# Two layers' norms with their short chains on GpSimd, and block-diagonal keys filled by 16 transfers a unit

## The chip, the cores and the metric

The kernel runs on one core of one Trainium2 chip (8 cores). A core has TensorE (PE, with its weight loads PEld), VectorE (DVE), ScalarE (ACT), GpSimd (POOL) and SyncE (SP, which issues transfers here). Each runs its own instructions in order, and semaphores tie them together. The metric is the device time of one execution in microseconds, the median of several.

## The reference

x is (16 sequences, 512 positions, 256 wide), and passes through six residual blocks, each on a layer-normed input:

```python
x = x + L0_attn(layernorm(x))    # rms norm, three gates by matmul, linear recurrence along positions, output matmul
x = x + L0_xattn(layernorm(x), ctx, ctx, mask)     # 16 heads of 16, 64 context keys
x = x + L0_ffn(layernorm(x))     # 256 -> 256 plus a rank-32 correction
x = x + L1_attn(layernorm(x))    # LSTM of width 20 over positions -> where to look, Gaussian weights, context
x = x + L1_xattn(layernorm(x), ctx, ctx, fside, mask)  # softmax times fside
x = x + L1_ffn(layernorm(x))     # each row goes to the best of 8 experts, 256 -> 128 -> 256

def _layernorm(x, eps=1e-05):
    return (x - mean(x)) / sqrt(var(x) + eps)

def _L0_attn_ref(x, norm_w, A_w, ...):
    xn = x * (norm_w / sqrt(mean(x * x) + EPS))
```

Scores, softmax and the sums are all in float32.

## The kernel before, in words

Positions are cut into 4 chunks of 128, sequences into 4 groups of 4; a chunk of a group is a unit (128 partitions x 4 sequences x 256). Each of the two layers has 16 units. Two lanes, each with its own tiles (names begin with l0 and l1, norms' tiles with ln0 and ln1; the profile leaves the numbers out), work on two units at once. Stages follow each other: in stages 0 and 1 both lanes run layer 0 (two bodies of two units each); in stages 2 and 3 lane 0 runs layer 0 and lane 1 layer 1 (four bodies each); in stage 4 lane 1 runs layer 1 (four bodies); in stage 5 both lanes run layer 1 (two bodies); stage 6 finishes the experts. The LSTM steps along the positions run beside stages 1 to 4: 64 steps a body in stage 1, 32 in stages 2 to 4. Each step is a chain of L942 on TensorE (slots in, gates out), L1109 and L1113 on ScalarE, and L1641 to L1649 on VectorE, which writes slots for the next step. The experts' tiles run in stages 4 to 6.

The order of the work is not written by hand. `norm_steps`, `attention_steps`, `layer0_steps` and others list steps (engine, family, index, cost in us, what it needs). `planned_at` (from L351) lists them out per engine by their costs and by the hop between engines, and `run_stages` emits each engine's share of that list. Where the plan has TensorE idle by over 0.3 us in stages 0 to 4 and 6, it puts in filler matmuls "warm" (L950), one for each 0.22 us of 0.9 of the gap. So a changed cost in a step changes the order on every engine, and the number of fillers.

A norm (each unit of layer 0 has four, of layer 1 two) is: statistics in two halves on VectorE (L1348 to L1353), variance plus epsilon on VectorE (L1357), the power −0.5 on GpSimd (L1697), the offset −mean x scale on VectorE (L1373), then two tiles normed by ScalarE (L1126) and two by VectorE (L1450). The first norm of layer 0 folds layernorm and rms norm in one scale and has `rms` (L1359 to L1369) and a second root between; its input is xin.

The scores of two sequences' heads are one matmul per half (L909): the queries against keys laid out block-diagonally, so that head e's 16 rows meet only its own 64 columns. Before, `load_context` (L726 to L742) loads plain keys kg (L737) once a unit, and GpSimd multiplies them with headmask into one of two 128x512 buffers kbd, eight times a unit (`keys`, L1712). GpSimd also adds the output's bias rows to the residual (`brow`, `frow`, `orow`, L1665), multiplies layer 1's exponents by fside (`gate`, L1719), copies rows for the LSTM's slots (L1677), and gathers rows for the experts. SyncE issues x, contexts, histories, stores and the experts' loads.

## Time and profile before

| what | value |
|---|---|
| time, median of 3 | 2620.91 us (2616.39 to 2623.07) |
| profiled execution, its time | 2631.95 us |
| its span | 2629.8 us |
| TensorE busy | 2302.6 us, 88% |
| VectorE, ScalarE, GpSimd busy | 60%, 54%, 40% |
| mean granted clock of TensorE | 0.947 |

The profile comes from one execution that is 11 us slower than the median. The span runs from the first to the last instruction. Busy time is a union of an engine's instructions; a filler counts as busy. From the timeline, the loop bodies end at about 220 and 355 us (stage 0), 524 and 692 (stage 1), 843, 986, 1130 and 1273 (stage 2), 1411, 1546, 1682 and 1820 (stage 3), 1930, 2032, 2138 and 2242 (stage 4), 2400 and 2560 (stage 5).

### The profile page before, as it was taken

To read this page: it belongs to the slowest core of one execution; us is meant where nothing else is said; L and a number is where in the kernel's file an instruction comes from. 1 tells how busy PE (TensorE), PEld (TensorE's weight loads), DVE (VectorE), ACT (ScalarE), POOL (GpSimd) and SP (SyncE) were. 2 spreads that over 40 slices of the span, in tenths; PEclk is the share of its full clock that TensorE was granted. 3 is DMA by queue.
4 is the path that set the end of the run, shared out by engine and by line. 5 is a ranking of instruction groups with operands and counts; after the bars stand their busy time and mean duration, and the time that the engine had idled before them with its cause. 6 is when DMAs were issued, how large, how long until landed. Compare 5 with 4: busy or idle time off the path is not lost.

```text
span 2629.8 us, 42733 instructions
## 1 busy us (share of the span) xinstructions
PE 2302.6 (88%) x11585; PEld 1499.8 (57%) x11585; DVE 1578.0 (60%) x5494; ACT 1425.8 (54%) x5145; POOL 1046.3 (40%) x1124
## 2 busy tenths in 40 slices
PE   5799999999899898989898989798888878697887
PEld 2365655656556564747465655556655546566664
DVE  4456477676665766666576767676645646364541
ACT  1263646658464554737474747464655646465632
POOL 0223241232233433333334343433555545487665
PEclk9899999999899999989899999998999999798989
DMA  4302020100302011111203030302353243353323
GB/s 161 99 11 64 14 62 1 51 9 1 94 9 70 17 53 35 46 49 30 48 17 94 1 95 0 86 16 81 103 126 97 78 121 90 112 163 98 92 62 105
DMA packets 203923, 168.32 MB, mean 64 GB/s; under 512 B 56847, under 2 KB 196717, under 8 KB 203452
## 3 DMA queue, kind: packets, MB, share of 16 engines
q1 hardware_dynamic: 189372, 140.73, 18.6%
q0 software_dynamic: 14336, 25.28, 3.3%
q8 instruction: 67, 1.10, 0.2%
q14 instruction: 148, 1.21, 0.2%
HBM read 125.11 MB, written 53.40 MB: 68 GB/s over the span
## 4 chain that ended last, share of the span: by engine, by line
PE 37%; issue 24%; DVE 16%; POOL 12%; ACT 5%; SPq 3%; DMA 2%; POOLq 0%; DVEq 0%; another core or an unknown queue 0%; ACTq 0%
PE p L970 7%; PE p L950 4%; PE p L873 4%; PE p L933 3%; PE p L909 3%; POOL l_scratch L1719 3%; PE p L867 3%; PE p L884 2%; PE pg L942 2%; PE p L923 2%; DVE l_xnat L1450 2%; POOL l_kbd L1712 2%; POOL l_xres L1665 2%; DVE ln_stats L1348 1%; PE p L1023 1%
## 5 line engine op out<-in xcount | busy, mean ns | idle before, releaser
L1161 ACT ACTIVATE l_scratch<-p,l_mx 128x64 f32<-128x64 f32 x2048 | 483.4, 323 | 30.8 <-DVE l_mx L1395 20.2
L950 PE MATMUL p<-warm 128*128 128x512 bf16 x1802 | 476.1, 394 | 1.2 <-DVE l_sums L1343 1.2
L1712 POOL TENSOR_TENSOR l_kbd<-l_kg,headmask 128x512 f32<-128x512 f32 x256 | 264.1, 1044 | 385.0 <-PE p L909 289.6
L942 PEld LDWEIGHTS pg<-slots,wcat 128*128 128x128 f32 x1024 | 174.7, 197 | 287.6 <-DVE slots L1649 218.6
L1697 POOL TENSOR_TENSOR ln_rstd<-ln_ve,neghalf 128x4 f32<-128x4 f32 x96 | 98.2, 1022 | 547.2 <-DVE ln_ve L1357 545.1
L942 PE MATMUL pg<-slots,wcat 128*128 128x16 f32 x1024 | 180.9, 252 | 125.7 <-DVE slots L1649 105.0
L933 PEld LDWEIGHTS p<-l_vg,l_scratch 128*128 128x128 f32 x2048 | 254.4, 193 | 62.3 <-ACT l_scratch L1169 37.7
L950 PEld LDWEIGHTS p<-warm 128*128 128x128 bf16 x1802 | 185.4, 107 | 173.5 <-issue 40.0
L933 PE MATMUL p<-l_vg,l_scratch 128*128 128x34 f32 x2048 | 264.0, 276 | 6.8 <-ACT l_scratch L1169 4.5
L909 PE MATMUL p<-l_kbd,l_qT 128*128 128x512 f32 x512 | 265.4, 600 | 0.6 <-POOL l_kbd L1712 0.5
L1719 POOL TENSOR_TENSOR l_scratch<-l_scratch,gp 128x512 f32<-128x512 f32 x128 | 162.5, 1270 | 221.3 <-DVE l_sums L1400 219.8
L1395 DVE TENSOR_REDUCE l_mx<-p 128x8 f32<-128x512 f32 x256 | 176.2, 690 | 93.9 <-PE p L909 86.8
L1641 DVE SCALAR_TENSOR_TENSOR pg<-gates,pg 20x16 f32<-20x16 f32 x512 | 89.8, 175 | 214.0 <-ACT gates L1109 194.1
L1109 ACT ACTIVATE gates<-pg 96x16 f32<-96x16 f32 x512 | 92.0, 180 | 219.9 <-PE pg L942 208.3
L867 PE MATMUL p<-ident,l_xnat 128*128 128x128 f32 x1024 | 158.4, 291 | 40.1 <-ACT l_xnat L1126 36.6
L1169 ACT ACTIVATE l_scratch<-p 128x512 f32<-128x512 f32 x256 | 153.6, 600 | 52.7 <-PE p L923 44.8
L1113 ACT ACTIVATE pg<-pg 20x16 f32<-20x16 f32 x512 | 77.3, 151 | 191.0 <-DVE pg L1645 179.5
L923 PE MATMUL p<-ident,l_scratch 128*128 128x128 f32 x1024 | 159.0, 282 | 22.7 <-DVE l_xnat L1410 16.8
L867 PEld LDWEIGHTS p<-ident,l_xnat 128*128 128x128 f32 x1024 | 124.6, 151 | 85.6 <-ACT l_xnat L1126 65.1
L1126 ACT ACTIVATE l_xnat<-l_xres,ln_shift,ln_rstd 128x256 f32<-128x256 f32 x160 | 87.1, 592 | 154.9 <-DVE ln_shift L1373 153.7
L923 PEld LDWEIGHTS p<-ident,l_scratch 128*128 128x128 f32 x1024 | 120.8, 148 | 81.2 <-issue 40.5
L1649 DVE SCALAR_TENSOR_TENSOR slots<-gates,pg 20x16 f32<-20x16 f32 x528 | 88.8, 171 | 104.8 <-ACT pg L1113 93.0
(281 smaller groups left out, 4381.7 us busy)
## 6 DMA issues: line engine op xcount, KB each, us to landing
xln<-xln_dram SPq DMA_DIRECT2D x40, 512.0 KB, 4.7
l_vg<-v_dram SPq DMA_DIRECT2D x32, 544.0 KB
x_dram<-l_xres SPq DMA_DIRECT2D x32, 512.0 KB, 4.2
l_kg<-k_dram SPq DMA_DIRECT2D x32, 256.0 KB
xln_dram<-l_xnat SPq DMA_DIRECT2D x16, 512.0 KB, 3.0
l_xres<-x_dram SPq DMA_DIRECT2D x16, 512.0 KB
x_dram<-l_xnat SPq DMA_DIRECT2D x16, 512.0 KB
xin<-in_x SPq DMA_DIRECT2D x12, 512.0 KB, 3.8
```

Source lines behind the costliest of these rows:

```text
L867: i = pe.transpose(banks[l][m][:, b * P:(b + 1) * P], src[:, b, m * P:(m + 1) * P], ident[:, :])
L909: pe.matmul(banks[l][j], w.qT[:, j, b * P:(b + 1) * P], w.kbd[b % 2][:, j, :, :].rearrange("p a k -> p (a k)"), start=False, stop=True).th ...
L923: i = pe.transpose(t_bank[l][:, p * P:(p + 1) * P], src, ident[:, :])
L933: i = pe.matmul(o_of(l, layer, c)[:, q * VW:(q + 1) * VW], w.exT[:, j, p, :], w.vg[:, b, q * VW:(q + 1) * VW], start=True, stop=True)
L942: pe.matmul(pg[:, 0:B], wcat[:, :], slots[:, s % STEPS, :], start=True, stop=True).then_inc(l_pe, 1)
L950: pe.matmul(banks[1][0] if layer > NC_ else px, warm[:, 0:P], warm[:, :], start=True, stop=True)
L970: i = pe.matmul(bank, w[:, k, half * P:(half + 1) * P], tiles[lane].xT[:, k, :], start=(k == 0), stop=(k == NH - 1))
L1161: i = act.activation(w.ex[b % 2][:, NE * j + h, :], banks[lane][j][:, h * SK:(h + 1) * SK], ACT.Exp, scale=-1.0, bias=w.mx[:, u % 4, h:h + 1])
L1169: act.activation(w.exT[:, i_ % 2, :, :], t_bank[lane].rearrange("p (a t) -> p a t", a=4), ACT.Identity).then_inc(t.exT, 1)
L1395: dve.tensor_reduce(w.mx[:, u % 4, :], banks[l][j].rearrange("p (a k) -> p a k", a=NE), AX_X, ALU.min).then_inc(t.top, 1)
L1712: pool.tensor_tensor(w.kbd[b % 2][:, j, :, :], w.kg[:, j, b:b + 1, :].broadcast_to([P, NE, SK]), headmask[:, :].rearrange("p (a o) -> p a ...
L1719: pool.tensor_tensor(ex, ex, gp[lane][:, b:b + 1, :].broadcast_to([P, NE, SK]), ALU.mult).then_inc(t.gated, 1)
```

## The change

What it does:

- All small operations of a norm between statistics and norm go to GpSimd: four for a plain norm (plus epsilon, power, mean x scale, x −1), eleven for layer 0's first. VectorE keeps statistics and its half of the norm.
- The plan's costs: 1.75 for a root with its chain and 4.2 for `rms` (before, 1.0 for a root, 1.2 for rms, 0.2 or 0.35 for the offset).
- kg, headmask and `keys` are gone. kbd is one tile of 128x4096 a lane, cleared once by VectorE at the start, and its diagonal blocks are written by 16 transfers a unit (one head of one half each: 16 partitions x 4 sequences x 64), 16 KB each. The score matmuls wait for them once a unit. The next context load now waits for all of the unit's scores.
- `brow` also waits for VectorE's half of the first norm; `orow` waits for the fourth score.
- Tiles move to make room: some of the experts' tiles lie in the columns of R, one of xg in the rows of the biases.

Filler matmuls in one body (first body of a stage / body of its loop), as the two programs have them:

| stage | before | after |
|---|---|---|
| 0 | 95 | 103 |
| 1 | 142 | 140 |
| 2 | 106 / 120 | 111 / 126 |
| 3 | 70 / 76 | 68 / 69 |
| 4 | 61 / 109 | 65 / 109 |
| 5 and 6 | 176 | 176 |

The diff, cut to its core:

```diff
+LOADS = (16 * (NE * NH + 1), 16 * (NE * NH + 2))
...
-        self.kg = sb(f"{name}_kg", [P, NH, GB, SK])
-        self.kbd = [sb(f"{name}_kbd{i}", [P, NH, NE, SK]) for i in range(2)]
+        self.kbd = sb(f"{name}_kbd", [P, GB, NH, NE, SK])
...
-    steps = [("dve", "stat", 2 * k + h, 1.2, after[h:h + 1]) for h in range(2)]
-    steps += [("pool", "root", k, 1.0, [("stat", 2 * k + 1)])]
-    if rms:
-        steps += [("dve", "rms", 0, 1.2, [("root", k)]), ("pool", "root", 9, 1.0, [("rms", 0)])]
-    steps += [("dve", "offset", k, 0.35 if rms else 0.2, [("root", 9 if rms else k)])]
-    steps += [("act", "norm", 2 * k, 1.2, [("offset", k)]), ("dve", "norm", 2 * k + 1, 1.0, [("offset", k)])]
+    steps = [("dve", "stat", 2 * k + h, 1.15, after[h:h + 1]) for h in range(2)]
+    steps += [("pool", "rms" if rms else "root", k, 4.2 if rms else 1.75, [("stat", 2 * k + 1)])]
+    ready = ("rms" if rms else "root", k)
+    steps += [("act", "norm", 2 * k, 1.2, [ready]), ("dve", "norm", 2 * k + 1, 1.0, [ready])]
...
-            ("pool", "keys", u, 1.07, [("score", u - 4)]),
-            ("pe", "score", u, 1.1, [("qland", u % 2), ("keys", u), ("neg", 0), ("exp", 4 * (u - 2) + 3)]),
+            ("pe", "score", u, 1.1, [("qland", u % 2), ("neg", 0), ("exp", 4 * (u - 2) + 3)]),
...
-    steps += [("pool", "orow", 0, 2.3, [("keys", 7)])]
+    steps += [("pool", "orow", 0, 2.3, [("score", 3)])]
...
-    steps += [("act", "base", 0, 2.4, [("rms", 0)]), ("pool", "brow", 0, 2.3, [("base", 0)]),
+    steps += [("act", "base", 0, 2.4, [("rms", 0)]), ("pool", "brow", 0, 2.3, [("base", 0), ("norm", 1)]),
...
-                    sp.wait_ge(t.kbd, 2 * GB * m)
+                    sp.wait_ge(t.scores, 2 * GB * m)
                     sp.wait_ge(t.pv, 2 * GB * m)
                     sp.wait_ge(t.neg, m)
                     if layer == 1 and m > LAYER0_UNITS[lane]:
                         sp.wait_ge(t.gated, 2 * GB * (m - LAYER0_UNITS[lane]))
                 sp.dma_start(w.vg[:, :, :], v_dram[layer, bass.ds(GB * g, GB), :, :].rearrange("b p n -> p b n")
                              ).then_inc(t.v_load, 16)
-                sp.dma_start(w.kg[:, :, :, :], k_dram[layer, :, :, bass.ds(GB * g, GB), :]).then_inc(t.m_load, 16)
+                for e in range(NE):
+                    rows = slice(HD * e, HD * e + HD)
+                    for h in range(NH):
+                        sp.dma_start(w.kbd[rows, :, h, e, :], k_dram[layer, rows, h, bass.ds(GB * g, GB), :]).then_inc(t.m_load, 16)
...
-                    pe.wait_ge(t.kbd, N + 1)
+                    if u == 0:
+                        pe.wait_ge(t.m_load, LOADS[0] * n + LOADS[0] if layer == 0 else LOADS[0] * LAYER0_UNITS[l] + LOADS[1] * n + LOADS[1])
                     pe.matmul(banks[l][j], w.qT[:, j, b * P:(b + 1) * P],
-                              w.kbd[b % 2][:, j, :, :].rearrange("p a k -> p (a k)"), start=False, stop=True
+                              w.kbd[:, b, j, :, :].rearrange("p a k -> p (a k)"), start=False, stop=True
...
-                    act.wait_ge(s.offset, s.before(layer, n, k) + 1)
+                    act.wait_ge(s.inv, s.before_roots(layer, n, k) + (4 if k else 8))
...
+            for t in tiles:
+                dve.memset(t.kbd[:, :, :, :, :], 0.0)
...
-            def rms(s, small, roots):
-
-                dve.wait_ge(s.inv, roots + 1)
-                dve.tensor_tensor(s.tmp[:, 0, :], s.rstd[:, 0, :], s.rstd[:, 0, :], ALU.mult).then_inc(s.small, 1)
-                dve.wait_ge(s.small, small + 6)
-                dve.tensor_tensor(s.tmp[:, 1, :], s.tmp[:, 0, :], s.mv[:, :, 1], ALU.mult).then_inc(s.small, 1)
-                dve.wait_ge(s.small, small + 7)
-                dve.tensor_scalar(s.ve[:, 1, :], s.tmp[:, 1, :], EPS, None, ALU.add).then_inc(s.small, 1)
-
-                dve.scalar_tensor_tensor(s.tmp[:, 2, :], s.mv[:, :, 0], -1.0, s.rstd[:, 0, :], ALU.mult, ALU.mult).then_inc(s.small, 1)
-                dve.tensor_scalar(s.tmp[:, 0, :], s.rstd[:, 0, :], 1.0, None, ALU.add).then_inc(s.small, 1)
...
-                dve.scalar_tensor_tensor(s.shift[:, :], s.mv[:, :, 0], -1.0, scale, ALU.mult, ALU.mult).then_inc(s.offset, 1)
...
-                    dve.wait_ge(s.offset, s.before(layer, n, k) + 1)
+                    dve.wait_ge(s.inv, s.before_roots(layer, n, k) + (4 if k else 8))
...
-                    elif i_ == 9:
-                        pool.wait_ge(s.small, s.before_small(0, n, 0) + 8)
-                        pool.tensor_tensor(s.rstd[:, 1, :], s.ve[:, 1, :], neghalf[:, :], ALU.pow).then_inc(s.inv, 1)
                     else:
-                        pool.wait_ge(s.small, s.before_small(layer, n, i_) + 5)
-                        if i_ == 0 and positive(n):
-                            pool.wait_ge(s.normed_act, s.before(0, n, 0))
-                            pool.wait_ge(s.normed_dve, s.before(0, n, 0))
+                        done = s.before_roots(layer, n, i_)
+                        pool.wait_ge(s.small, s.before_small(layer, n, i_) + 4)
+                        pool.tensor_tensor(s.ve[:, 0, :], s.mv[:, :, 1], eps4[:, :], ALU.add).then_inc(s.inv, 1)
+                        pool.wait_ge(s.inv, done + 1)
                         pool.tensor_tensor(s.rstd[:, 0, :], s.ve[:, 0, :], neghalf[:, :], ALU.pow).then_inc(s.inv, 1)
+                        pool.wait_ge(s.inv, done + 2)
+                        pool.tensor_tensor(s.tmp[:, 1, :], s.mv[:, :, 0], s.rstd[:, 0, :], ALU.mult).then_inc(s.inv, 1)
+                        pool.wait_ge(s.inv, done + 3)
+                        pool.tensor_tensor(s.shift[:, :], s.tmp[:, 1, :], minus4[:, :], ALU.mult).then_inc(s.inv, 1)
+                elif family == "rms":
+                    done = s.before_roots(0, n, 0)
+                    pool.wait_ge(s.small, s.before_small(0, n, 0) + 4)
+                    if positive(n):
+                        pool.wait_ge(s.normed_act, s.before(0, n, 0))
+                        pool.wait_ge(s.normed_dve, s.before(0, n, 0))
+                        pool.wait_ge(l0.base_ready, n)
+                    pool.tensor_tensor(s.ve[:, 0, :], s.mv[:, :, 1], eps4[:, :], ALU.add).then_inc(s.inv, 1)
+                    pool.wait_ge(s.inv, done + 1)
+                    pool.tensor_tensor(s.rstd[:, 0, :], s.ve[:, 0, :], neghalf[:, :], ALU.pow).then_inc(s.inv, 1)
+                    pool.wait_ge(s.inv, done + 2)
+                    pool.tensor_tensor(s.tmp[:, 0, :], s.rstd[:, 0, :], s.rstd[:, 0, :], ALU.mult).then_inc(s.inv, 1)
+                    pool.wait_ge(s.inv, done + 3)
+                    pool.tensor_tensor(s.tmp[:, 1, :], s.tmp[:, 0, :], s.mv[:, :, 1], ALU.mult).then_inc(s.inv, 1)
+                    pool.wait_ge(s.inv, done + 4)
+                    pool.tensor_tensor(s.ve[:, 1, :], s.tmp[:, 1, :], eps4[:, :], ALU.add)
+                    pool.tensor_tensor(s.tmp[:, 3, :], s.mv[:, :, 0], minus4[:, :], ALU.mult).then_inc(s.inv, 1)
+                    pool.wait_ge(s.inv, done + 5)
+                    pool.tensor_tensor(s.rstd[:, 1, :], s.ve[:, 1, :], neghalf[:, :], ALU.pow).then_inc(s.inv, 1)
+                    pool.wait_ge(s.inv, done + 6)
+                    pool.tensor_tensor(s.tmp[:, 4, :], s.rstd[:, 0, :], s.rstd[:, 1, :], ALU.mult).then_inc(s.inv, 1)
+                    pool.wait_ge(s.inv, done + 7)
+                    pool.tensor_tensor(s.shift[:, :], s.tmp[:, 3, :], s.tmp[:, 4, :], ALU.mult).then_inc(s.inv, 1)
+                    pool.tensor_tensor(s.tmp[:, 2, :], s.tmp[:, 3, :], s.rstd[:, 0, :], ALU.mult).then_inc(s.inv, 1)
+                    pool.tensor_tensor(s.tmp[:, 0, :], s.rstd[:, 0, :], minus4[:, :], ALU.subtract).then_inc(s.inv, 1)
                 elif family == "brow":
                     pool.wait_ge(l0.base_ready, n + 1)
+                    pool.wait_ge(s.normed_dve, s.before(0, n, 0) + 1)
...
+                    pool.wait_ge(t.scores, 2 * GB * m + 4)
...
-                elif family == "keys":
-                    if i_ == 0:
-                        pool.wait_ge(t.m_load, 32 * n + 32 if layer == 0 else 32 * LAYER0_UNITS[lane] + 48 * n + 48)
-                    if positive(N - 3):
-                        pool.wait_ge(t.scores, N - 3)
-                    pool.tensor_tensor(
-                        w.kbd[b % 2][:, j, :, :], w.kg[:, j, b:b + 1, :].broadcast_to([P, NE, SK]),
-                        headmask[:, :].rearrange("p (a o) -> p a o", o=1).broadcast_to([P, NE, SK]), ALU.mult
-                    ).then_inc(t.kbd, 1)
```

How the order changes, first on GpSimd, at the head of a loop body of stage 2 (l0 is layer 0's lane, l1 layer 1's; ln0 is lane 0's norm; L1697 and L1691 are the two roots of the first norm, L1665 is the first row addition). Before:

```order
L1712 TENSOR_TENSOR l0_kbd0<-l0_kg,headmask 128x512
...
L1697 TENSOR_TENSOR ln0_rstd<-ln0_ve,neghalf 128x4
...
L1734 TENSOR_TENSOR l1_scratch<-l1_scratch,below 128x512
...
L1712 TENSOR_TENSOR l1_kbd0<-l1_kg,headmask 128x512
...
L1691 TENSOR_TENSOR ln0_rstd<-ln0_ve,neghalf 128x4
L1712 TENSOR_TENSOR l0_kbd0<-l0_kg,headmask 128x512
...
L1712 TENSOR_TENSOR l1_kbd1<-l1_kg,headmask 128x512
...
L1665 TENSOR_TENSOR l0_xres<-l0_xres,rowOut 128x1024
...
L1677 COPY slots<-R 96x128
L1712 TENSOR_TENSOR l0_kbd1<-l0_kg,headmask 128x512
L1712 TENSOR_TENSOR l1_kbd1<-l1_kg,headmask 128x512
...
L1688 TENSOR_TENSOR pos1_nrm<-pos1_nrm,neghalf 128x4
```

After:

```order
L1650 COPY slots<-R 96x128
...
L1679 TENSOR_TENSOR ln0_ve<-ln0_mv,eps4 128x4
...
L1681 TENSOR_TENSOR ln0_rstd<-ln0_ve,neghalf 128x4
...
L1683 TENSOR_TENSOR ln0_tmp<-ln0_rstd 128x4
...
L1685 TENSOR_TENSOR ln0_tmp<-ln0_tmp,ln0_mv 128x4
...
L1687 TENSOR_TENSOR ln0_ve<-ln0_tmp,eps4 128x4
...
L1690 TENSOR_TENSOR ln0_rstd<-ln0_ve,neghalf 128x4
...
L1692 TENSOR_TENSOR ln0_tmp<-ln0_rstd 128x4
...
L1694 TENSOR_TENSOR ln0_shift<-ln0_tmp 128x4
...
L1726 TENSOR_TENSOR l1_scratch<-l1_scratch,below 128x512
...
L1650 COPY slots<-R 96x128
...
L1638 TENSOR_TENSOR l0_xres<-l0_xres,rows0 128x1024
```

Before, five key products stand between the roots and around the row addition; afterwards the chain runs in one piece, behind two slots copies, and the row addition comes later than it.

On VectorE, the same place: from the mask's conversion to the norm of xin. pg, uin and slots are the LSTM's. Before:

```order
L1387 TENSOR_SCALAR l0_neg<-mask8_0 128x256
...
L1362 TENSOR_TENSOR ln0_tmp<-ln0_rstd 128x4
...
L1364 TENSOR_TENSOR ln0_tmp<-ln0_tmp,ln0_mv 128x4
...
L1366 TENSOR_SCALAR ln0_ve<-ln0_tmp 128x4
L1368 SCALAR_TENSOR_TENSOR ln0_tmp<-ln0_mv,ln0_rstd 128x4
L1369 TENSOR_SCALAR ln0_tmp<-ln0_rstd 128x4
...
L1641 SCALAR_TENSOR_TENSOR pg<-gates,pg 20x16
...
L1458 TENSOR_TENSOR ln0_tmp<-ln0_rstd 128x4
...
L1373 SCALAR_TENSOR_TENSOR ln0_shift<-ln0_mv,ln0_tmp 128x4
...
L1450 TENSOR_SCALAR l0_xnat<-xin,ln0_mv,ln0_tmp 128x256 x2
```

After:

```order
L1371 TENSOR_SCALAR l0_neg<-mask8_0 128x256
...
L1374 TENSOR_SCALAR l1_neg<-mask32_1 128x256
...
L1614 SCALAR_TENSOR_TENSOR pg<-gates,pg 20x16
...
L1616 SCALAR_TENSOR_TENSOR uin<-gates,pg 20x16
...
L1618 SCALAR_TENSOR_TENSOR pg<-pg,uin 20x16
L1622 SCALAR_TENSOR_TENSOR slots<-gates,pg 20x16
...
L1432 TENSOR_SCALAR l0_xnat<-xin,ln0_mv,ln0_tmp 128x256 x2
```

The rms chain and the offset between the mask's conversion and the norm are gone; one LSTM step stands between them.

On SyncE, the loads of the first two units ahead of the first loop body. Before:

```order
L724 DMA xin<-in_x 128x4x256
L735 DMA l0_vg<-v_dram 128x4x272
L737 DMA l0_kg<-k_dram 128x2x256
L739 DMA mask8_0<-in_mask0 128x4x64
L724 DMA xln1<-in_x 128x4x256
...
L737 DMA l1_kg<-k_dram 128x2x256
```

After:

```order
L720 DMA xin<-in_x 128x4x256
L731 DMA l0_vg<-v_dram 128x4x272
L736 DMA l0_kbd<-k_dram 16x4x64 x16
L738 DMA mask8_0<-in_mask0 128x4x64
L720 DMA xln1<-in_x 128x4x256
...
L736 DMA l1_kbd<-k_dram 16x4x64 x16
```

The load of lane 1's x (xln1) now stands behind 16 key transfers of lane 0 instead of one.

## Rows read from the trace of the kernel before

**Rows 1.** The profile page, part 1: busy time and share of each engine.

```profile
PE 2302.6 (88%) x11585; PEld 1499.8 (57%) x11585; DVE 1578.0 (60%) x5494; ACT 1425.8 (54%) x5145; POOL 1046.3 (40%) x1124
```

**Rows 2.** Windows, one loop body each: length, busy (instructions) by engine, clock, DMA share, GB/s.

```profile
220.00:355.00 135.00, 133.87 (x627) 83.42 (x626) 76.74 (x230) 73.82 (x212) 41.51 (x33) 1.00 0.15 47
524.00:692.00 168.00, 160.72 (x785) 98.83 (x784) 118.78 (x482) 104.44 (x402) 42.06 (x37) 1.00 0.11 33
986.00:1130.00 144.00, 129.59 (x641) 82.60 (x640) 92.42 (x317) 80.66 (x302) 50.79 (x46) 0.95 0.15 41
1546.00:1682.00 136.00, 121.92 (x608) 79.31 (x606) 94.44 (x317) 82.96 (x303) 50.69 (x47) 0.95 0.15 46
2032.00:2138.00 106.00, 87.93 (x480) 58.00 (x479) 60.07 (x232) 57.53 (x231) 54.81 (x70) 0.97 0.34 99
2400.00:2560.00 160.00, 131.66 (x680) 95.82 (x679) 74.15 (x229) 84.07 (x262) 104.29 (x126) 0.88 0.30 84
```

**Rows 3.** Groups by line and form: busy us, mean ns, idle before, releasers.

```profile
L1712 POOL TENSOR_TENSOR l_kbd<-l_kg,headmask 128x512 f32<-128x512 f32 x256 | 264.1, 1044 | 385.0 <-PE p L909 289.6 <-DMA mask<-in_mask 95.2
...
L1719 POOL TENSOR_TENSOR l_scratch<-l_scratch,gp 128x512 f32<-128x512 f32 x128 | 162.5, 1270 | 221.3 <-DVE l_sums L1400 219.8
...
L1697 POOL TENSOR_TENSOR ln_rstd<-ln_ve,neghalf 128x4 f32<-128x4 f32 x96 | 98.2, 1022 | 547.2 <-DVE ln_ve L1357 545.1
...
L1450 DVE TENSOR_SCALAR l_xnat<-l_xres,ln_mv,ln_rstd 128x256 f32<-128x256 f32 x160 | 63.0, 436 | 2.0
...
L1450 DVE TENSOR_SCALAR l_xnat<-xin,ln_mv,ln_tmp 128x256 f32<-128x256 f32 x24 | 51.4, 2183 | 1.0
...
L1373 DVE SCALAR_TENSOR_TENSOR ln_shift<-ln_mv,ln_rstd 128x4 f32<-128x4 f32 x80 | 31.0, 387 | 35.3 <-POOL ln_rstd L1697 33.2
...
L1754 POOL TENSOR_TENSOR held<-neghalf 1x1 f32<-1x1 f32 x96 | 17.8, 185 | 54.7 <-DVE xy L1607 52.5 <-issue 0.8
```

**Rows 4.** Timeline of 976 to 1016 us: start, duration, instruction, [idle before <-releaser].

```profile
975.70 4.48 PE L950 MATMUL p<-warm 128*128 128x512 bf16 x20
...
980.18 2.68 DVE L1373 SCALAR_TENSOR_TENSOR ln_shift<-ln_mv,ln_rstd 128x4 f32<-128x4 f32 x1 [3.63 <-POOL ln_rstd L1697]
980.80 2.03 POOL L1712 TENSOR_TENSOR l_kbd<-l_kg,headmask 128x512 f32<-128x512 f32 x2
...
990.62 1.01 POOL L1697 TENSOR_TENSOR ln_rstd<-ln_ve,neghalf 128x4 f32<-128x4 f32 x1 [7.78 <-DVE ln_ve L1357]
...
996.51 0.29 DVE L1387 TENSOR_SCALAR l_neg<-mask 128x256 bf16<-128x256 uint8 x1
...
1002.40 5.72 DVE L1450 TENSOR_SCALAR l_xnat<-xin,ln_mv,ln_tmp 128x256 f32<-128x256 f32 x2
...
1009.16 0.60 PE L942 MATMUL pg<-slots,wcat 128*128 128x16 f32 x2 [4.34 <-DVE slots L1649]
...
1014.85 1.53 PE L970 MATMUL p<-l_xT,wD 128*128 128x512 f32 x3
```

**Rows 5.** Timeline of VectorE before the first loop body.

```profile
2.65 4.27 DVE L1268 MEMSET xg<- 128x512 f32 x8
...
28.52 0.61 DVE L1281 TENSOR_SCALAR wA<-wA,normw 128x256 f32<-128x256 f32 x2 [12.39 <-DMA wms<-in_W_mu_sig]
```

**Rows 6.** Timeline of the start of the first loop body, 84 to 110 us.

```profile
85.50 0.62 SPq L737 DMA_DIRECT2D l_kg<-k_dram  x1
...
86.83 0.55 SPq L724 DMA_DIRECT2D xln<-in_x  x1
...
93.04 0.75 DVE L1348 BATCH_NORM_STATS2 ln_stats<-xln 128x6 f32<-128x256 f32 x2 [9.99 <-DMA xln<-in_x]
...
95.61 2.04 POOL L1712 TENSOR_TENSOR l_kbd<-l_kg,headmask 128x512 f32<-128x512 f32 x2 [95.17 <-DMA mask<-in_mask]
...
105.08 0.48 DVE L1387 TENSOR_SCALAR l_neg<-mask 128x256 bf16<-128x256 uint8 x2
```

**Rows 7.** Timeline of SyncE's queue, the context loads of stage 2.

```profile
1094.82 0.53 SPq L737 DMA_DIRECT2D l_kg<-k_dram  x1
```

58 lines of the change are left out of this document (22 added, 36 removed).

## The prediction

> **What bounds the kernel now.** I read the busy shares first, then each stage's loop body by windows, then the timeline of one body engine by engine, and the groups by line last. TensorE is busy for 2302.6 of 2629.8 us [rows 1]. That is an average. A body of stage 0 leaves it idle for 1.1 us of 135, one of stage 1 for 7.3 of 168, of stage 2 for 14.4 of 144, of stage 3 for 14.1 of 136, of stage 4 for 18.1 of 106, of stage 5 for 28.3 of 160 (length less busy time, [rows 2]). And its busy time is not all work: the planner puts filling matmuls into gaps that it expects, 0.22 us each (20 in 4.48 us, [rows 4]), and an in-order engine does them whether the gap comes or not. So the time moves only by (a) waits inside the idle microseconds, (b) the number of fillers, and (c) the run up to the first body. GpSimd is busy for 40%, VectorE for 60% [rows 1]: neither is the bound by its sum. They matter by latency, where one norm's chain stands before TensorE's next work.
>
> One such place is the head of a stage-2 body [rows 4]. The root is through at 991.63 (990.62 + 1.01), the norm by VectorE starts at 1002.40 and takes 5.72 us for two tiles, where the same form on xres takes 0.44 us each [rows 3], so about 4.85 us are a stall. Because VectorE is stuck there, the LSTM's cell update comes late, and TensorE waits for 4.34 us at 1009.16. The norm's user, the wD product, runs at 1014.85. What stands on GpSimd there are key products, the row addition and a copy for the LSTM's slots (the order of before is in the section on the change). The same shape stands at 980.18: an operation on 4 columns takes 2.68 us on VectorE, beside two key products on GpSimd that together take 2.03 us; the group's mean is 0.387 [rows 3].
>
> That is a rule of the Trainium skill too, "SBUF — State Buffer", section "SBUF: two separate sides": VectorE and GpSimd share a pair of ports under an exclusive lock held for the whole instruction, so the loser is blocked and not slowed. The 2.68 us above agrees for operations with two SBUF inputs. By that rule alone, GpSimd's removed keys free VectorE, while its new short operations block it by at most one short operation at a time.
>
> **The change, part by part.** The sum is against the profiled execution: 2629.8 us span, 2631.95 us its time, 11 above the median 2620.91.
>
> *1. Keys off GpSimd.* 256 products of 1.044 us go, 264.1 us in all [rows 3], 8.3 per unit. They were seldom waited for by TensorE itself; their worth is that VectorE is no longer blocked and that roots and row additions no longer queue behind them.
>
> *2. The norm's chain onto GpSimd.* A plain norm has 4 operations there, the first norm of layer 0 has 11. Roots keep 1.022 us each [rows 3]. The price of a 128x4 product there is in no row. The nearest are 1x1 in 0.185 and 128x512 in 1.044 [rows 3]: (1044 − 185) / 511 = 1.7 ns a column, so 0.19 us for 4 columns. The low end is 0.185, the high end is that of the 128x4 power, 1.022. I take 0.19, since power is the odd operation. With a hop of some 0.05 us each, a plain chain is 1.02 + 3 × 0.24 = 1.7 us, and the first norm's 2 × 1.02 + 9 × 0.24 = 4.2. Before, VectorE's part cost 0.17 to 1.23 us an operation with stalls and needed a hop between engines each time. Unstalled, a plain norm is therefore even or 0.2 us later; where VectorE was occupied it is earlier. The first norm of the stage-2 body: from root through (991.63) to norm (1002.40) 10.8 us go down to about 3.2, plus what stands before it.
>
> *3. What that gives TensorE per body.* Stage 2 and 3: the 4.34 us wait goes, and of the 2.68 us stall 2.5 go, 6.8 in all; one us comes back as fillers change and something else is late next (the LSTM's own chain, 32 steps a body, whose gates, cell and slots hop between three engines and stay as they are). I take −6 a body. The low end is −1.5 (the LSTM hides nearly all), the high end −10 of the 14 idle. Eight bodies: −48 (−80 to −12). Fillers in the two stages' bodies: stage 2 from 106 and 120 to 111 and 126, stage 3 from 70 and 76 to 68 and 69 (the counts in the two programs, first and further bodies): +1.3 and −1.5 us a body, which nearly cancel and are in the −6.
> Stage 1: 7.3 us idle a body, −4 each, −8 (−16 to 0). Stage 0: no idle time to win, and 8 more fillers a body × 0.22 = 1.8 us each: +3 (0 to +7), less than the full 3.5 because a filler may stand where TensorE would wait. Stage 4: the experts' weights and the row gathers share SyncE's queue and the DMA engines (share 0.34, [rows 2]); +1 a body, +4 (−6 to +14). Stage 5: gate products of 1.270 us [rows 3] stay on GpSimd, keys go, 28.3 us idle: −3 a body, −6 (−18 to +6).
>
> *4. Row additions.* The first now waits for VectorE's norm 1. Behind it on GpSimd stand the position root and the next norm's chain, so a late VectorE norm delays them; by point 2 that norm is 7 us earlier, so I price this at nothing. If the cover is gone, it costs what the norm is late: 1 to 2 us a body.
>
> *5. Loads.* One load of the keys, 0.62 us to issue [rows 6], becomes 16. The issue alone of the 15 more is at 0.44 (0.53 to 0.62 for rows of whole tiles [rows 6, 7], a little less for small ones, an estimate) 6.6 us of SyncE per unit; ends 0.4 and 0.67: 6 and 10. In the loop it is hidden: the context of stage 2's next body is issued at 1094.82 [rows 7] and its first reader, the mask's conversion, ran at 996.51 in this body [rows 4], hence about 1140 in the next, 45 us later. At the start it isn't. Lane 0's key load is issued at 85.50, lane 1's x at 86.83, and VectorE's first statistics wait 9.99 us for that x until 93.04 [rows 6]. They will start about 6.6 us later. Then GpSimd did two key products before the root (2.04 us at 95.61), which are gone: +4.6. I take +5 (+4 to +9). VectorE's mask conversion at 105.08 comes 16 issues of either lane later, about 107, which the shifted start hides.
>
> The 16 transfers are 16 KB each, in pieces of 256 bytes where the old had 1 KB. Against this speaks a rule of the Trainium skill, "DMA: Bandwidth & Descriptors", section "Rules for kernel authors": coalesce small transfers, since under 64 KB most of the time is overhead. No row here shows such a transfer. What it would do to this kernel is rival B.
>
> *6. The memsets.* Two of 128x4096 on VectorE, less one of 128x512. At 4.27 us for 8 of 128x512 [rows 5] that is 15 × 0.53 = 8.0 us. They stand before a wait of 12.39 us for the last weight load [rows 5], which hides them (one load fewer there, 0.4 us earlier): 0. Uncovered they would cost 8.
>
> **The sum.** +5 + 3 − 8 − 48 + 4 − 6 = −50: 2631.95 → 2582 profiled, 2571 on the scale of the median.
>
> **The rivals.**
> *Rival A, hidden.* TensorE's order, the fillers and the LSTM set the time, and other waits take the place of the 4.34 us. For it: most of the wait in a body is for the slots of the LSTM, and stage 0 gets longer. Against: the wait at 1009.16 ends by an operation queued behind the blocked norm. Eight bodies at −1.5 are −12, stage 1 and 5 give 0, the start +5, stage 0 +3, stage 4 +4: 0, or 2621; with stages 1 and 5 at half their terms −7, or 2614.
> *Rival B, the queue, slower.* In stage 4 and 5 SyncE also issues the experts' loads, x loads and stores. Each unit adds 15 issues. If a small transfer backs the queue up to over 1 us per issue, 16 us stand ahead of the x load and the experts' weights, and TensorE waits for them. Place: stage 4's four bodies (16 us × 4 = 64 at most, some 40 uncovered), the start (+15), stage 5 (+12); the rest of the sum remains: 40 + 15 + 12 on 2571 is 2638. It decides from about 1 us per issue. Against: 0.62 us was the price of the 256 KB one.
> *Rival C, dear small operations.* GpSimd's 4-column product costs about 1 us like its power. A plain chain is then 4.2 us and the first norm's 11.7, so a unit's norms come 3 × 2.5 + 7.5 = 15 us later in all. If 3 of these 15 are exposed, 32 units give +96 on 2571: 2667. Against: the 1x1 product's 0.185.
>
> **How the numbers follow.** What a measurement of this kernel can tell from no change is 0.3%, 8 us. Forecast (2545 to 2600) 0.60; a larger gain, all idle time of stages 2 to 3 and more in 5, under 2545, 0.12; rival A 0.14, of which 0.05 still faster by over 8 us and 0.09 within; rival B 0.09; rival C 0.05. Faster 0.77, same 0.09, slower 0.14. The range 2530 to 2616 leaves out the slower cases, a part of A and the end of the large gain; the forecast's own range is 2545 to 2600.
>
> **What would show each step.** GpSimd's busy time falls from 1046 to about 860 us (−264, + some 77 for the small operations). A 4-column product there takes about 0.19 us; over 0.5 makes C right. VectorE's norm pair on xin takes under 1 us in place of 5.7. TensorE's 4.34 us wait for slots at the head of stage 2's bodies is gone, and bodies of stage 2 take 136 to 139 us, stage 3 129 to 132. Stage 0's bodies are 135 to 137. The first body starts VectorE's statistics near 99 to 100 us. An issue of a key load takes 0.4 to 0.6 us; near 1 or above, or bodies of stage 4 over 110 us, makes B right. If the norm comes earlier but the body stays at 143, A is right: the prediction fails at step 3.

## The result and the profile after

The changed kernel takes 2524.41 us (median of 4, 2518.01 to 2531.20), the kernel before beside it 2618.65: the ratio is 0.9629, with a 95% interval of 0.9589 to 0.9669. That is 94 us less; the forecast was 50 less, and the range ended at 2530. Against the profiled executions the span goes from 2629.8 to 2521.2, 108.6 us; the profiled run of before took 13 us more than its median and that of the changed kernel 1 us less, so 94 is the size of the effect, and the terms measured below, which come from this pair, hold some 14 us of spread.

The page's busy times, to be read against [rows 1]:

```profile
PE 2267.1 (90%) x11601; PEld 1481.2 (59%) x11601; DVE 1414.4 (56%) x5209; ACT 1420.0 (56%) x5145; POOL 862.1 (34%) x1252
```

GpSimd goes from 1046.3 to 862.1, as forecast (860). VectorE loses 163.6 us. TensorE, whose work is the same, loses 35.5 us of busy time with 16 instructions more, all of them fillers.

Windows over the whole of stage 2, 3, 4 and 5 with 6, kernel before and then after; the columns are those of [rows 2]:

```profile
692.90:1273.00 580.10, 521.75 (x2574) 335.71 (x2575) 371.87 (x1286) 322.26 (x1206) 203.24 (x184) 0.94 0.15 40
1273.00:1820.00 547.00, 488.27 (x2454) 322.68 (x2455) 374.32 (x1265) 330.25 (x1210) 199.60 (x181) 0.95 0.17 47
1820.00:2241.90 421.90, 350.13 (x1908) 235.40 (x1908) 242.46 (x948) 230.97 (x923) 220.41 (x280) 0.95 0.35 100
2241.90:2629.80 387.90, 315.44 (x1617) 222.54 (x1616) 166.13 (x475) 187.49 (x590) 254.27 (x331) 0.88 0.38 107
```

```profile
695.00:1243.80 548.80, 505.15 (x2595) 327.23 (x2595) 332.13 (x1220) 319.64 (x1208) 156.72 (x215) 0.97 0.17 44
1243.80:1743.20 499.40, 469.05 (x2432) 314.44 (x2432) 317.91 (x1194) 327.42 (x1210) 152.59 (x212) 0.98 0.18 52
1743.20:2145.90 402.70, 354.63 (x1911) 236.09 (x1912) 227.05 (x932) 231.47 (x923) 194.43 (x273) 0.94 0.38 104
2145.90:2521.20 375.30, 307.31 (x1616) 217.87 (x1616) 151.26 (x459) 187.45 (x590) 226.46 (x323) 0.89 0.39 111
```

Term by term, in the profiled pair:

| part | forecast | measured |
|---|---|---|
| start and stage 0 | +5 +3 | +6.1 (355.9 to 362.0) |
| stage 1 | −8 | −4.0 (337.0 to 333.0) |
| stages 2 and 3 | −48 | −31.3 and −47.6 |
| stage 4 | +4 | −19.2 |
| stages 5 and 6 | −6 | −12.6 |
| sum | −50 | −108.6 |

Stages 2 and 3 show two things. Idle time of TensorE (length less busy) falls from 58.4 to 43.7 and from 58.7 to 30.4 us, 43 in all. And 5028 instructions before and 5027 after take 1010.0 and 974.2 us: 36 us less for the same work, while the granted clock of the two stages rises from 0.94 and 0.95 to 0.97 and 0.98 of the full 2.4 GHz. The clock alone would make of the 1010.0 us some 979 (521.75 × 0.94 / 0.97 and 488.27 × 0.95 / 0.98, an estimate from these rows), so it accounts for nearly all of the 36. This second part stood in no term of the sum.

The loop bodies of stage 2 alone, before and after:

```profile
986.40:1129.70 143.30, 128.89 (x639) 82.31 (x638) 92.42 (x317) 80.41 (x301) 50.79 (x46) 0.95 0.15 40
1129.70:1273.00 143.30, 131.45 (x642) 83.83 (x641) 91.84 (x328) 80.54 (x301) 48.08 (x42) 0.93 0.15 44
```

```profile
965.30:1105.60 140.30, 127.09 (x645) 81.03 (x646) 82.45 (x299) 79.92 (x301) 39.27 (x54) 0.96 0.16 41
1105.60:1243.80 138.20, 125.67 (x646) 80.51 (x645) 84.11 (x309) 79.92 (x301) 38.50 (x52) 0.98 0.17 45
```

Here TensorE's idle time has hardly moved (14.4 and 11.9, now 13.2 and 12.5): of the 3.0 and 5.1 us that a body lost, 1.8 and 5.8 are busy time. The idle time went in the first two bodies of the stage (32.1 us before 986.4, 17.9 before 965.3) and in stage 3.

The groups that answer to [rows 3], columns as there:

```profile
L1669 POOL TENSOR_TENSOR ln_tmp<-ln_mv,ln_rstd 128x4 f32<-128x4 f32 x80 | 16.1, 201 | 6.3
...
L1432 DVE TENSOR_SCALAR l_xnat<-xin,ln_mv,ln_tmp 128x256 f32<-128x256 f32 x24 | 9.9, 455 | 10.6 <-POOL ln_shift L1694 9.4 <-DMA xln_dram<-l_xnat 0.7
```

A 4-column product on GpSimd takes 0.201 us, for which 0.19 had been taken. The norm of xin on VectorE takes 0.455 us a tile and not 2.183. What stood beside it in the kernel before are these rows of GpSimd at the head of the stage-2 body, where the norm ran from 1002.40 to 1008.12 [rows 4]:

```profile
1002.21 2.36 POOL L1665 TENSOR_TENSOR l_xres<-l_xres,rowOut 128x1024 f32<-128x1024 f32 x1
...
1004.93 3.04 POOL L1712 TENSOR_TENSOR l_kbd<-l_kg,headmask 128x512 f32<-128x512 f32 x3
```

With a copy of 0.46 us between them they cover the norm from start to end: the first row addition is 2.36 of these 5.72 us, and not only the key products held VectorE up. All eight bodies of stages 2 and 3 had this norm at 5.7 us. The head of a body of stage 2, timeline, to be read against [rows 4]:

```profile
970.55 1.01 POOL L1681 TENSOR_TENSOR ln_rstd<-ln_ve,neghalf 128x4 f32<-128x4 f32 x1
...
973.97 0.20 POOL L1694 TENSOR_TENSOR ln_shift<-ln_tmp 128x4 f32<-128x4 f32 x1
...
976.41 0.61 PE L942 MATMUL pg<-slots,wcat 128*128 128x16 f32 x2 [6.56 <-DVE slots L1622]
...
976.59 1.35 DVE L1374 TENSOR_SCALAR l_neg<-mask 128x256 bf16<-128x256 int32 x1
...
979.03 0.74 DVE L1432 TENSOR_SCALAR l_xnat<-xin,ln_mv,ln_tmp 128x256 f32<-128x256 f32 x2
...
981.92 0.45 PE L942 MATMUL pg<-slots,wcat 128*128 128x16 f32 x2
```

From the first root's end (971.56) to the norm 7.5 us pass instead of 10.8, and the chain itself is done at 974.17; what stands before the norm is VectorE's own queue, the LSTM's step that waits for the first 942 of the body. TensorE's wait for slots at the second has gone (981.92 without one), as forecast. But the wait at the first 942, 3.76 us in the same place of before, has grown to 6.56 (976.41). Its slots wait for ScalarE, which in the trace stands idle for 5.52 us with nothing but "issue" ahead of it at the head of this body, 2.93 before. The conversion at 976.59 shows that the stall's kind has not gone: it takes 1.35 us beside an operation of GpSimd (L1726) that runs from 976.45 for 1.35 us, and took 0.29 in the kernel before. So in this body one wait took the place of another, and what I had allowed for that was 1 us.

The start, timeline, against [rows 6]:

```profile
86.77 7.70 SPq L736 DMA_DIRECT2D l_kbd<-k_dram  x16
...
99.14 0.75 DVE L1352 BATCH_NORM_STATS2 ln_stats<-xln 128x6 f32<-128x256 f32 x2 [14.83 <-DMA xln<-in_x]
...
105.66 0.50 DVE L1371 TENSOR_SCALAR l_neg<-mask 128x256 bf16<-128x256 uint8 x2 [2.40 <-DMA mask<-in_mask]
```

Sixteen issues take 7.70 us, 0.48 each, and lane 1's x is issued behind them, at 94.98. The first statistics start at 99.14, in the forecast's 99 to 100.

### The profile page after: what moved, and what is told of

Its sections match the earlier page's. It is cut to its first block, busy times and chain, and to the rows that moved or that the text cites. A ratio compares the mean times of both kernels' runs of the same rounds, so it can differ in the third digit from the quotient of the medians.

```text
span 2521.2 us, 43111 instructions
## 1 busy us (share of the span) xinstructions
PE 2267.1 (90%) x11601; PEld 1481.2 (59%) x11601; DVE 1414.4 (56%) x5209; ACT 1420.0 (56%) x5145; POOL 862.1 (34%) x1252
## 4 chain that ended last, share of the span: by engine, by line
PE 45%; issue 18%; DVE 12%; POOL 10%; ACT 7%; SPq 3%; DMA 3%; POOLq 0%; another core or an unknown queue 0%; DVEq 0%; ACTq 0%
PE p L970 6%; PE p L909 5%; PE p L933 5%; PE p L950 5%; PE p L872 4%; PE p L883 3%; PE p L923 3%; PE p L866 3%; PE p L1023 2%; POOL l_scratch L1711 2%; PE pg L942 2%; DVE ln_stats L1352 2%; ACT l_scratch L1161 2%; PE p L906 1%; POOL id_dram L1720 1%
## 5 line engine op out<-in xcount | busy, mean ns | idle before, releaser
L1665 POOL TENSOR_TENSOR ln_ve<-ln_mv,eps 128x4 f32<-128x4 f32 x80 | 16.0, 200 | 613.0 <-DVE ln_mv L1357 612.9
L866 PEld LDWEIGHTS p<-ident,l_xnat 128*128 128x128 f32 x1024 | 119.5, 146 | 104.5 <-ACT l_xnat L1126 69.3
L1144 ACT ACTIVATE l_xT<-p 128x512 f32<-128x512 f32 x192 | 108.2, 596 | 60.1 <-PE p L866 57.7
```

The source lines that it names most:

```text
L866: i = pe.transpose(banks[l][m][:, b * P:(b + 1) * P], src[:, b, m * P:(m + 1) * P], ident[:, :])
L1144: act.activation(w.xT[:, h, :], banks[lane][h], ACT.Identity).then_inc(ln[lane].landed, 1)
```

## The experiments

Ratios are to the kernel before on the same chip, with 95% intervals. Chips differ by up to 0.9% in the kernel before (2618.65 to 2642.01), and the ratio of the changed kernel differs with them: 0.9629 and 0.9628 on two chips, 0.9675 on two others where the kernel before is slower (2636 and 2642 us). So only runs of one chip can be compared below 12 us. These were run together: norms_only, keys_only, keys_in_plan, no_fillers_23; after_again, keys_32, x_first_keys_8, brow_early; keys_in_plan_2, side_products, side_memsets, best; after_3, keys_only_2, masks_first; after_4, keys_masks_first. All profiles are of single executions.

**The two halves of the change alone.** norms_only is the kernel before with these parts of the diff (GpSimd's chains, their plan costs, the wait of the first row addition), keys_only is the kernel before with the rest.

```diff
 norms_only:  headmask, kg, two kbd buffers and the step "keys" stay
 keys_only:   rms and offset on VectorE, root 1.0, two roots for the first norm stay
```

> The kernel before with only the norms' chains moved to GpSimd; the keys are still multiplied there. Theory 1 (VectorE was held up beside GpSimd's key products, and that delayed norms and LSTM steps): the chain no longer hops to VectorE, so the long stalls of 4-column operations go, but a plain chain can now queue behind a 1.04 us product and VectorE's two-tile norm of xin still lies beside the products: it keeps over half of its 2.18 us. About a third of the gain of 94 us, 2580 to 2600. Theory 2 (the chain's hops between the engines were what cost, the products were harmless): nearly all of the gain, 2525 to 2545, and VectorE's norm of xin falls to about 0.45 us here too.

> The kernel before with only the keys loaded to their places by 16 transfers; VectorE keeps its part of the norms' chains. Theory 1: over half of the gain of 94, 2545 to 2575; the two-tile norm of xin falls from 2.18 to about 0.45 us a tile, and the offset's mean from 0.387 to under 0.25. Theory 2: under 30 us faster than before, 2590 or more. In both, the start is some 5 us later than before, as in the changed kernel.

Measured: norms_only 0.9925 (0.9905 to 0.9945), 21 us faster; keys_only 0.9645 (0.9622 to 0.9668), 94 us faster. VectorE's norm of xin, group by form, in each:

```profile
L1428 DVE TENSOR_SCALAR l_xnat<-xin,ln_mv,ln_tmp 128x256 f32<-128x256 f32 x24 | 25.0, 1080 | 13.7 <-POOL ln_shift L1690 13.4
```

```profile
L1454 DVE TENSOR_SCALAR l_xnat<-xin,ln_mv,ln_tmp 128x256 f32<-128x256 f32 x24 | 14.8, 659 | 0.8
```

The keys carry the gain, and theory 2 is out. Theory 1 was right in direction; it gave the norms too much (a third of the gain; 21 of 94 us came) and the keys too little (2545 at best; 94 us is all of the gain). The offset's mean in keys_only is 0.219 us, as expected, but the norm of xin stays above the 0.45. The rest of it stands in three bodies of stage 3, beside the first row addition, which is free to run there:

```profile
1361.56 2.35 POOL L1669 TENSOR_TENSOR l_xres<-l_xres,rows 128x1024 f32<-128x1024 f32 x1 [0.28 <-ACT l_xres L1138]
...
1361.81 2.65 DVE L1454 TENSOR_SCALAR l_xnat<-xin,ln_mv,ln_tmp 128x256 f32<-128x256 f32 x2
```

In stage 2 of the same run it takes 0.41 us a tile. So the 2.18 us were made of the products and the row addition: norms_only has the products left and makes it 1.08, keys_only the row addition and makes it 0.66.

**The plan.** keys_in_plan is the changed kernel, planned with the key steps, which then do nothing, so that its order is that of norms_only.

```diff
+            ("pool", "keys", u, 1.07, [("score", u - 4)]),
-            ("pe", "score", u, 1.1, [("qland", u % 2), ("neg", 0), ("exp", 4 * (u - 2) + 3)]),
+            ("pe", "score", u, 1.1, [("qland", u % 2), ("keys", u), ("neg", 0), ("exp", 4 * (u - 2) + 3)]),
-    steps += [("pool", "orow", 0, 2.3, [("score", 3)])]
+    steps += [("pool", "orow", 0, 2.3, [("keys", 7)])]
...
+                elif family == "keys":
+                    pass
```

> The changed kernel, planned as if the key products were still there (the plan's step and its waits stay, GpSimd does nothing at it), so that the order of work is that of the run with only the norms changed. Theory 1 (the time comes from the work that is gone): within 12 us of the changed kernel, 2515 to 2540. Theory 3 (the new plan's order and its fillers bring part of it): 2545 or more, with the bodies of stage 3 over 128 us against 123 to 125.

> The changed kernel planned with the key products' steps, at which GpSimd does nothing, once more: the base for the next two, which have its order of work. All theories: 0.967 of the kernel before, within 0.004.

0.9674 (0.9655 to 0.9694), and again 0.9671 (0.9646 to 0.9697) against 0.9629 and 0.9628 for the changed kernel on other chips. By these ratios the new order would bring 11 us, but the changed kernel did not run on these two chips, and on two others it has 0.9675 itself. So the new order brings 0 to 12 us, and that is not settled. With the order held, the missing products bring 0.9925 to 0.9674 on one chip: 2.5%, 65 us.

**Products beside VectorE.** In stages 0 to 3 GpSimd does one operation at each of these steps into a tile that is idle there (xg), 192 in all; no engine waits for it. The base is keys_in_plan_2.

```diff
 side_products:
+                    pool.tensor_tensor(out_, ident[:, 0:SK] (broadcast), rank (broadcast), ALU.mult)   # 128x512
 side_memsets:
+                    pool.tensor_tensor(xg[3 + lane][0:1, 0:1], neghalf[0:1, 0:1], neghalf[0:1, 1:2], ALU.mult)
+                    for z in range(2):
+                        pool.memset(xg[3 + lane][:, 1 + z * D:D + z * D], 0.0)
```

> The same, and in stages 0 to 3 GpSimd does at each of these steps (192 in all) one product of the old form and size into a tile that nobody reads there; TensorE waits for none. Theory 1a (VectorE is held up beside GpSimd's operations that read two inputs): VectorE's busy time in stages 1 to 3 grows by over 25 us with the same instructions, its norm of xin goes from 0.53 to over 0.9 us a tile; the whole is 25 to 60 us slower than the base. Theory 1b (what counts is that the norms' chains and row additions queue behind the products on GpSimd): slower by as much, but VectorE's busy time stays within 10 us. Theory 2 (the products were harmless beside the rest of the change): within 8 us of the base.

> As the run before, with clearing writes (1x1 product, then two of 128 by 256 and 255 columns, some 0.6 to 1.0 us together) in place of the product. It occupies GpSimd, but reads no tile of VectorE's size. Theory 1a: VectorE's busy time stays within 10 us of the base, the norm of xin near 0.53, and the time is 0 to 15 us over the base, well under that of the products. Theory 1b: slower than the base in the ratio of the occupied time, two thirds or more of what the products cost.

Measured: products 0.9745 (0.9719 to 0.9771), 20 us over the base; memsets 0.9701 (0.9676 to 0.9727), 8 us over it, with intervals of the ratios that overlap. The busy row of the page and the norm of xin, base, products, memsets:

```profile
PE 2264.6 (89%) x11431; PEld 1488.7 (59%) x11574; DVE 1409.3 (56%) x5209; ACT 1419.6 (56%) x5145; POOL 864.5 (34%) x1252
```

```profile
L1433 DVE TENSOR_SCALAR l_xnat<-xin,ln_mv,ln_tmp 128x256 f32<-128x256 f32 x24 | 12.0, 542 | 11.3 <-POOL ln_shift L1695 10.9
```

```profile
PE 2264.8 (89%) x11431; PEld 1485.0 (58%) x11574; DVE 1452.6 (57%) x5209; ACT 1420.3 (56%) x5145; POOL 1061.1 (42%) x1444
```

```profile
L1719 POOL TENSOR_TENSOR xg<-ident,rank 128x512 f32<-128x512 f32 x192 | 200.0, 1051 | 311.7 <-PE p L911 226.6 <-DVE l_sums L1349 82.0 <-PE pg L944 0.8
...
L1434 DVE TENSOR_SCALAR l_xnat<-xin,ln_mv,ln_tmp 128x256 f32<-128x256 f32 x24 | 23.7, 1028 | 12.6 <-POOL ln_shift L1696 12.2
```

```profile
PE 2269.5 (89%) x11431; PEld 1491.0 (59%) x11574; DVE 1420.9 (56%) x5209; ACT 1421.9 (56%) x5145; POOL 996.4 (39%) x1828
```

```profile
L1719 POOL MEMSET xg<- 128x255 f32 x384 | 105.4, 301 | 0.0
...
L1434 DVE TENSOR_SCALAR l_xnat<-xin,ln_mv,ln_tmp 128x256 f32<-128x256 f32 x24 | 15.1, 671 | 12.1 <-POOL ln_shift L1696 11.7
```

With the same VectorE instructions, 192 products of 1.051 us add 43 us to its busy time and double the norm of xin; the memsets, with 146 us of GpSimd's time against the products' 200, add 11.6. In proportion to the time that GpSimd is occupied, the memsets cost VectorE about a third as much. But they are not harmless: theory 1a's marks for them (under 10 us, the norm of xin near 0.53) were both missed, and VectorE's copies into R show it, in the base and beside the memsets:

```profile
L1627 DVE TENSOR_SCALAR R<-slots 32x128 f32<-32x128 f32 x28 | 8.1, 290 | 1.0
```

```profile
L1628 DVE TENSOR_SCALAR R<-slots 32x128 f32<-32x128 f32 x28 | 12.7, 454 | 1.0
```

Beside the products they take 0.492 us. An operation with two large inputs behaves otherwise: the product that writes l_qT (128x512) takes 0.686 us in the base, 0.738 beside the products and 0.686 beside the memsets. So VectorE is held up beside an operation of GpSimd that reads; its one-input operations, most of what stretches here, are held up beside one that only writes too. The rule of the Trainium skill, "SBUF — State Buffer", section "SBUF: two separate sides", has both cases: the lock is between any GpSimd operation and a VectorE operation in a 2-port mode (one that takes the pair of ports which the two engines share), and, for a VectorE operation with two SBUF inputs, only against a GpSimd operation that reads. The trace agrees for the two-input product; that the one-input operations ran in such a mode is shown by no row, but their stretching beside the memsets fits it.

In total time the products cost 20 us, less than the 25 that both theories had named for them, and the memsets 8: 41% of it, under theory 1b's two thirds. So theory 1a is shown for VectorE's busy time and is the likelier one for the total, where the memsets' 8 us are not clear of the spread. Up to the end of stage 3 the products cost 28.4 us in the profile (1749.7 to 1778.1), and between keys_in_plan and norms_only, on another chip, 21.1 (1751.4 to 1772.5): in these stages their presence is the whole effect within the spread. In stages 2 and 3 the profiled pair loses 20.5 us, of which 11.7 are idle time of TensorE and 8.8 a longer busy time for the same instructions, at a granted clock of 0.96 and 0.94 against 0.97 and 0.95. The other part of the 65 us lies in stages 4 to 6.

**The clock.** no_fillers_23 is the changed kernel without filler matmuls in stages 2 and 3.

```diff
-IDLE, FILL, WARM = 0.3, 0.9, (0, 1, 2, 3, 4, 6)
+IDLE, FILL, WARM = 0.3, 0.9, (0, 1, 4, 6)
```

> The changed kernel without filler matmuls in stages 2 and 3. It tells how much of the missed gain may lie in TensorE's granted clock: from the kernel before to the changed one, the clock of stages 2 and 3 rose from 0.94 to 0.97. If the clock weighs (theory 4), TensorE's idle time grows, the granted clock of these stages falls below 0.8, its work apart from the fillers takes over 60 us longer there, and the whole comes to 2560 or more. If the clock is harmless since TensorE waits for the LSTM anyway, the time stays within 12 us of 2524.

0.9951 (0.9934 to 0.9968): of a gain of 3.3 to 3.7% only 0.5% is left. Windows of stages 2 and 3 in it:

```profile
694.70:1291.40 596.70, 468.68 (x2106) 341.03 (x2107) 332.07 (x1220) 321.19 (x1208) 156.63 (x215) 0.81 0.16 41
1291.40:1818.30 526.90, 442.21 (x2156) 313.40 (x2156) 318.03 (x1194) 328.32 (x1210) 152.39 (x212) 0.89 0.17 49
```

The clock falls to 0.81 and 0.89, not below 0.8 as expected, and 4262 instructions without fillers take 911 us; the changed kernel's 5027 took 974, of which 765 are fillers. At 0.22 us these are 168 us, so the other work takes 806 there and 911 here, 105 us more (an estimate, as the 0.22 is). The fall of the clock alone would make 926 of the 806 (398 × 0.97 / 0.81 and 408 × 0.98 / 0.89), so it is enough to explain them. The clock can weigh as much as all else in this change, and it must be a term.

The change's own 36 us of clock do not hang on the products alone: norms_only, which still has them, runs stages 2 and 3 at 0.97 and 0.96, and its TensorE is busy there for 977 us against 1010, some 7 of these 33 us by 33 fillers fewer.

**The queue.** keys_32 cuts each transfer in two; x_first_keys_8 makes 8 of them and loads both lanes' x first.

```diff
 keys_32:
+                        for q in range(0, GB, 2):
+                            sp.dma_start(w.kbd[rows, q:q + 2, h, e, :], k_dram[layer, rows, h, bass.ds(GB * g + q, 2), :])
 x_first_keys_8:
+        k_dram = nc.dram_tensor("k_dram", [2, P, B, NH, SK], ...)
+                    sp.dma_start(w.kbd[rows, :, :, e, :], k_dram[layer, rows, bass.ds(GB * g, GB), :, :])
             for lane in range(2):
                 load_x(lane, 0, lane, 0)
+            for lane in range(2):
                 load_context(lane, 0, 0, lane, 0)
```

> The changed kernel once more, on the chip of the three runs below, so that they can be compared with it. All theories: 0.963 of the kernel before, within 0.004.

> The changed kernel with each of the 16 key transfers cut in two (32 of 8 KB a unit). Theory queue (the issues and the small transfers cost, my rival B): 16 more issues of 0.48 us, 7.7 us, stand ahead of the next x load, history or experts' load in each unit; stages 4 and 5 get longer by over 15 us together and the start by 7.7: slower than the changed kernel by over 20 us. Theory hidden (only the start sees the queue): slower by 7.7 at the start and otherwise within 5 us: +5 to +13.

> The changed kernel with 8 key transfers of 32 KB a unit (both halves of a head in one; for that the keys lie with the halves inside the sequences in DRAM) and with both lanes' x loaded ahead of their contexts at the start. By my term for the start (15 issues ahead of lane 1's x) the first statistics come 7 to 8 us earlier, near 91.5 us against 99.1. Theory hidden: 5 to 9 us faster than the changed kernel and not more. Theory queue: 15 to 30 us faster, since 8 issues less a unit also free stages 4 and 5.

after_again 0.9628 (0.9604 to 0.9653), keys_32 0.9883 (0.9861 to 0.9905), x_first_keys_8 0.9634 (0.9613 to 0.9656). From 16 to 32 transfers costs 64 us, from 16 to 8 gives nothing: from the end of stage 0 on, x_first_keys_8 takes 2165.4 us and after_again 2165.5. For the start it is no clean test, since its keys are stored to DRAM in twice as many transfers ahead of the first body, and lane 1's x is issued only at 91.68. VectorE's norm of xin in keys_32, and TensorE's windows of the start with stage 0, stage 2 and stage 4 in keys_32 and then in after_again:

```profile
L1433 DVE TENSOR_SCALAR l_xnat<-xin,ln_mv,ln_tmp 128x256 f32<-128x256 f32 x24 | 9.1, 421 | 16.8 <-DMA xln_dram<-l_xnat 11.0 <-POOL ln_shift L1695 3.2 <-POOL ln_tmp L1696 2.4
```

```profile
84.50:376.50 292.00, 260.99 (x1199) 163.64 (x1209) 121.80 (x374) 140.13 (x411) 62.43 (x104) 0.95 0.14 37
...
709.70:1267.90 558.20, 502.81 (x2559) 327.06 (x2596) 332.20 (x1220) 320.21 (x1208) 156.94 (x215) 0.97 0.17 43
...
1776.20:2196.90 420.70, 354.10 (x1886) 236.80 (x1912) 227.02 (x932) 231.74 (x923) 193.47 (x271) 0.94 0.38 104
```

```profile
84.50:361.30 276.80, 259.68 (x1199) 163.38 (x1208) 121.81 (x374) 140.04 (x411) 62.51 (x104) 0.97 0.16 44
...
694.50:1241.00 546.50, 503.58 (x2559) 328.09 (x2596) 332.14 (x1220) 320.11 (x1208) 157.00 (x215) 0.98 0.17 44
...
1744.30:2149.70 405.40, 354.56 (x1886) 240.55 (x1912) 227.53 (x932) 232.36 (x923) 194.87 (x273) 0.94 0.37 104
```

It costs 15 us at the start, 12 in stage 2, 15 in stage 4. The releaser "DMA xln_dram" says how in layer 0's units: the norm waits for a store of its tile that stands in SyncE's queue behind the key transfers. In stage 4, which has no norm of xin, GpSimd's waits for the experts' weights that land in the tile xin grow from 17.6 to 39.2 us. This is rival B, and it decides at 15 us of issues a unit, not at the 7.7 of the change; its sum was 67 us, though with 40 in stage 4. The Trainium skill, "DMA: Bandwidth & Descriptors", section "Rules for kernel authors", would coalesce transfers this small; the trace agrees at 8 KB and 32 a unit, and shows no price at 16 KB and 16 in the loop.

**The first row addition.**

```diff
-                    pool.wait_ge(s.normed_dve, s.before(0, n, 0) + 1)
-("pool", "brow", 0, 2.3, [("base", 0), ("norm", 1)])
+("pool", "brow", 0, 2.3, [("base", 0)])
```

> The changed kernel with the first row addition free to run before VectorE's half of the norm, as in the kernel before (in the plan too). Theory 1 (GpSimd's long operations hold VectorE's two-tile norm up): the norm of xin goes from 0.455 back to over 0.9 us a tile, as it lies beside a 2.35 us row addition in some units; the time grows by 3 to 15 us. If the norm stays at 0.45 and the time within 4 us, this wait did nothing.

0.9620 (0.9597 to 0.9642) beside 0.9628, and the norm of xin at 0.453: in this order of work the row addition does not meet the norm, and the wait did nothing. In the order of keys_only it does meet it, in the three bodies shown above.

**The start.** best loads both x first and has the row addition free (diffs above). masks_first also loads both masks of layer 0 ahead of values and keys, and gives the masks a semaphore of their own.

```diff
+            for lane in range(2):
+                sp.dma_start(mask8[lane][:, :, :], unit(a["mask0"], 0, lane)).then_inc(at[lane].mask_load, 16)
-                        dve.wait_ge(t.m_load, LOADS[0] * n + LOADS[0])
+                        dve.wait_ge(t.mask_load, 16 * n + 16)
```

> The changed kernel with both lanes' x loaded ahead of their contexts at the start, and the first row addition free again. By the start's term 7 to 8 us come off (first statistics near 91.5 us, 16 issues of 0.48 us earlier), the row addition gives 0 to 3: 0.959 to 0.961 of the kernel before, against 0.963.

> The changed kernel with x, then both masks of layer 0 loaded ahead of values and keys, and a semaphore of their own for the masks. In the run best VectorE's statistics came at 90.56 but its mask conversion still waited for lane 1's mask, behind the keys, until 104.91, and VectorE's norms behind it. If that wait was what held the start, the conversion now comes before 96 us and the first stage ends 5 to 8 us earlier, 355 us or less against 361; the whole 0.960 to 0.961 of the kernel before. If not, no change.

best 0.9646 (0.9620 to 0.9672), 7 us less than keys_in_plan_2 on its chip; the changed kernel did not run there, and no gain over its 0.9628 to 0.9675 is shown. Its stage 0 ends at 360.8, as before. In its timeline the statistics come 8.6 us earlier, and the mask's conversion, at the same time as before, holds up VectorE's norms behind it; then the same of masks_first:

```profile
90.56 0.75 DVE L1353 BATCH_NORM_STATS2 ln_stats<-xln 128x6 f32<-128x256 f32 x2 [7.03 <-DMA xln<-in_x]
...
104.91 0.49 DVE L1372 TENSOR_SCALAR l_neg<-mask 128x256 bf16<-128x256 uint8 x2 [10.23 <-DMA mask<-in_mask]
```

```profile
89.30 0.75 DVE L1356 BATCH_NORM_STATS2 ln_stats<-xln 128x6 f32<-128x256 f32 x2 [7.24 <-DMA xln<-in_x]
...
99.81 0.73 DVE L1436 TENSOR_SCALAR l_xnat<-xin,ln_mv,ln_tmp 128x256 f32<-128x256 f32 x2 [3.53 <-POOL ln_shift L1698]
```

In masks_first stage 0 ends at 352.4 against 360.6 in after_3 on the same chip, the 5 to 8 us expected, though the whole was to come to 0.960 or 0.961. It is 0.9660 (0.9640 to 0.9679) against 0.9675 (0.9657 to 0.9694), 6 us by medians, within the intervals. Moving the masks alone was not run.

**The chains on GpSimd once the products are gone.**

> The changed kernel on the chip of the next two. All theories: 0.963 of the kernel before, within 0.004.

> Only the keys changed, VectorE keeps its part of the chains; now on one chip with the changed kernel. Theory A (the chains on GpSimd add nothing once the products are gone): within 6 us of the changed kernel. Theory B (they bring stage 4 its gain, since there the run with the keys alone still had TensorE wait 28 us for ScalarE's copies of the gathered rows, against 6 in the changed kernel): 8 to 25 us slower than the changed kernel, 10 or more of it in stages 4 and 5, and faster than it in stage 2.

keys_only_2 0.9640 (0.9621 to 0.9659), 10 us faster than after_3 by medians, with intervals that just touch; the profiled pair lies 19 us apart. Windows of stages 2 to 4, after_3 and then keys_only_2:

```profile
693.70:1242.90 549.20, 507.05 (x2595) 328.59 (x2596) 332.15 (x1220) 319.55 (x1208) 156.71 (x215) 0.97 0.17 44
1242.90:1745.70 502.80, 470.29 (x2431) 314.61 (x2432) 317.43 (x1194) 327.41 (x1210) 152.62 (x212) 0.97 0.18 51
1745.70:2160.80 415.10, 358.63 (x1911) 238.83 (x1912) 229.51 (x932) 231.34 (x923) 194.37 (x273) 0.94 0.37 101
```

```profile
686.60:1220.80 534.20, 498.68 (x2564) 324.33 (x2565) 334.46 (x1286) 320.61 (x1206) 138.01 (x120) 0.97 0.18 47
1220.80:1737.70 516.90, 483.54 (x2469) 318.39 (x2469) 342.63 (x1265) 327.06 (x1210) 135.68 (x118) 0.97 0.18 50
1737.70:2147.90 410.20, 354.94 (x1924) 238.78 (x1923) 229.97 (x948) 229.44 (x923) 186.85 (x248) 0.94 0.37 102
```

In this pair the chains on GpSimd gain 14.1 us in stage 3 and lose 15.0 in stage 2, 3.8 in stage 1 and some 5 each in stage 4 and in 5 with 6. keys_only on its own chip has the same lengths in stages 1 to 3 (329.4, 534.4, 519.0), so these differences hold; the two of 5 us may be spread. Much of the two large ones is the plan's fillers: keys_only_2 has 456 in stage 2 where the changed kernel has 489, and 314 in stage 3 where it has 275. At 0.22 us each that is 7 of the 15.0 us and 9 of the 14.1. Theory B is out: stage 4's gain does not come from the chains. Theory A's 6 us were missed too, on the other side: the chains cost 10 by medians.

**Both findings together.** keys_masks_first is keys_only with masks_first's edits.

> The changed kernel on the chip of the next one: 0.963 to 0.968 of the kernel before.

> Only the keys changed (VectorE keeps its part of the chains), with x and the masks loaded ahead of values and keys. If what keys_only_2 and masks_first showed adds up: 8 us off at the start on top of 0.964, so 0.961 of the kernel before, 5 to 17 us faster than the changed kernel, stage 0 ending near 350 us.

keys_masks_first takes 2535.65 us, 0.9605 (0.9572 to 0.9639), beside 0.9675 (0.9637 to 0.9713) for the changed kernel there: 17 us less by medians, faster than both kernels. Its slowest execution (2541.64) is below the fastest of the changed kernel (2548.31). Stage 0 ends at 349.5 us.

## Why the prediction was wrong

The step that failed is step 3, "what that gives TensorE per body": the sum had −50, and 94 us went. It had no term for TensorE's clock (36 us in stages 2 and 3), and its terms for stages 4 and 5 came to −2 where −32 was measured. The direction, the start, GpSimd's busy time, the small operations' price and the hidden memsets came out as worked; the size did not.

1. *Keys off GpSimd and "what that gives TensorE per body" (steps 1 and 3), −48 where −79 was measured.* The mechanism, VectorE held up beside the products, is shown (side_products). The size was taken from one wait in one body. In just this body only 1.2 us of idle time went; all bodies of the two stages together gave 43 us, which lies near the 48 by luck, since it went in other places than the one read, and 36 us came as a faster clock for the same instructions. That term was missing, and no_fillers_23 shows that the clock can be worth some 105 us in these stages. The bodies of stage 3, for which 129 to 132 us had been named, take 123 and 125. The reading of the one body was short, too: of the 5.72 us, 2.36 stood beside the first row addition and not beside key products, and ahead of the two key products beside the 2.68 us stood two copies for the slots (980.11, 0.72 us).
2. *Stage 4, +4 where −19 was measured, and stage 5, −6 where −13 was.* I had taken SyncE's queue as the cost and left out that the products stood beside the norms there too. With the order held, keys_in_plan's stage 4 takes 414.3 us (1751.4 to 2165.7) and norms_only's 441.3 (1772.5 to 2213.8). The same 938 instructions of VectorE are busy there for 229 us and for 249: the mask's conversion takes 2.06 us instead of 0.29, and a scan of 8 numbers 4.90 instead of 0.16, beside two copies and four key products of GpSimd. So the blocking is at work in stage 4 as well. How much of the 27 us is blocking and how much the queue on GpSimd was not separated: the side runs stop at stage 3.
3. *The norm's chain (step 2).* Its price was right, 1.7 and 4.2 us, but I had counted the earlier norm as its gain. It gains 21 us while the products are there and loses some 10 once they are gone. Two cures for one stall were in the change, and the sum did not ask which one makes the other idle.
4. *The start (step 5), +5 with stage 0's +3.* Measured +6.1. The cause was half right: the x and the mask both stand behind the keys; moving x alone gives nothing back, moving both gives the 8 us. I had said of the mask that the shifted start hides it.
5. *Rival B* needs twice the issues that the change has. *Rival C* is out at 0.20 us; its sum was too high besides, since it gave the four norms of layer 0 to the 16 units of layer 1, which have two. *Rival A* has a grain of truth in the loop bodies of stage 2, which came to 140.3 and 138.2 us with the same idle time as before.

Open: how the 27 us of stage 4, and the products' cost in stages 5 and 6, divide between blocking and GpSimd's queue; how much of the 36 us of clock follows from the 43 us of idle time (with the products put back, clock and idle time lose about alike); why the clock in norms_only is higher too; and what makes the part of the chains' loss in stage 2 (about half) and of their gain in stage 3 (some 40%) that is not fillers.

## What to carry to other kernels

Where one engine's short operations stretch (2.7 us for 4 columns), look at what the neighbour runs then, and price the removal of that neighbour over every stage in which the two overlap, not at the one stall that shows best. For an engine at 88% busy with a granted clock below 1, put a term for the clock beside the term for idle time: same instructions, fewer microseconds. When a change holds two cures for one stall, run each alone before keeping both.

## What the runs showed of the hardware

- 192 products of 128x512 on GpSimd whose results nobody uses added 43 us to VectorE's busy time, 0.23 us each; 384 memsets of 128 by 256 or 255 in their place, with 192 products of one element, added 11.6.
- The hold-up counts as busy time of the operation held up: a norm of two tiles took 5.72 us in place of 0.74, a scan of 8 numbers 4.90 in place of 0.16, each about as long as the unbroken work of GpSimd beside it.
- VectorE's one-input copies into R stretched beside memsets as well (0.290 to 0.454 us), its two-input product for l_qT only beside products (0.686 to 0.738).
- Transfers of 8, 16 and 32 KB issue at 0.47, 0.48 and 0.49 us each (15.08 us for 32, 7.70 for 16, 3.89 for 8), one of 256 KB at 0.62: the issue is paid by count.
- SyncE's key issues were free in the loop at 7.7 us a unit and cost 64 us in 2525 at 15.
- Without the 765 fillers of stages 2 and 3 the granted clock was 0.81 in stage 2 and 0.89 in stage 3, where the changed kernel has 0.97 and 0.98, and the kernel was some 3% slower (0.9951 of the kernel before against 0.9628 to 0.9675).
